# A two-layer graph network kernel: the weight sums, the scales and the second row tile are reordered in the first stage

## The chip, the cores and the metric

The kernel runs on one core of one Trainium2 chip. The metric is the device time of one execution in microseconds (us), the median over several executions. A core has five engines that run their own instruction streams and meet at semaphores: TensorE (PE, matrix products and transposes), VectorE (DVE), ScalarE (ACT), GpSimd (POOL) and SyncE (SP, which here only issues transfers).

## The reference

2500 nodes with 1024 features, 80,000 edges with weights, two 1024 x 1024 weight matrices:

```python
edge_index = jnp.stack([src, dst])
h = jnp.maximum(_layernorm(x, axis=-1), 0.0)
# first layer: support = h @ W0; out[dst] += support[src] * edge_weight
x = x + _L0_gnn_ref(h, L0_gnn_W, edge_weight, src, dst)
h = jnp.maximum(_layernorm(x, axis=-1), 0.0)
# second layer: (h @ W1.T + b), summed over edges and self loops, scaled by degrees
x = x + _L1_gnn_ref(h, edge_index, L1_gnn_W, L1_gnn_b)
return x
```

## The kernel before

The nodes are 20 row tiles of 128. The first stage computes, for each row tile t, `support = h @ W0`. A 32-bit factor is split into two 16-bit parts, a high one (`hi`) and what is left of it (`lo`), and each product is three: hi x hi, hi x lo, lo x hi. Later stages turn the edge list into dense 128-column weight tiles by one-hot products, multiply them with the support, and do the second layer in the same way. There is no planner: each engine's order is written out by hand, one block for each engine, and the order of the calls in a block is the order of the engine's queue.

The start of the kernel matters here. Its steps, with the names of the code:

- **SP** issues the load of tiles 0 and 1 of x (`load_x(0)`), of the edge weights, destinations and sources (640 for each of 125 partitions), of W0 in four pieces into `w_nat` (semaphores `w0nat_in`), and later the other groups of x.
- **DVE** computes the moments of tiles 0 and 1 (`moments(0)`, `scale_shift(0)`), the largest edge weight, and from the integer lists two fields `field[0]` and `field[1]`. Then it makes a power-of-two scale for the edge weights (`wscale`), the scaled edge weights `w_s` with the high part `w_hi` (`field[2]`) and the left-over `w_lo` (`field[3]`), and from the largest row sum of W0 a scale for W0 (`powers`, semaphore `w_pow`). For each of the eight blocks k of 128 rows of W0 it makes the low part (L890), when ACT has made the high part (L1483). After the eight, it runs two scans over one row (L896, L897, semaphore `scans_ready`), and the moments of tiles 4 to 7.
- **ACT** takes the square root of the variances (`std`), normalizes a row tile and makes its high part (`rows_normal`, L1411 and L1416), sums the absolute values of W0's rows (`weight_sums`, L1443), copies transposed tiles out of PSUM (`transposed`, L1423), copies transposed fields out of PSUM (`field_out`, L1455), and makes the high parts of W0 (L1483).
- **POOL** makes the low part of a normalized row tile (`h_left`, L687), and after the scans three conversions (L693 to L696) ahead of `h_left(2)`.
- **PE** transposes the row tiles (`transpose_rows`, L1617) and the fields (`turn_field`, L1592), turns a column of 128 maxima into a row (`spread_max`, L1577), sends a value to all partitions (`to_all`, L1582), computes the support (`support`, L1634: six products of 128x512 for each block k), and spreads the scans (`spread_scans`, L1604).

What PE does for tile 0 stands in this order:

```python
            for t in range(T):
                support(t, 0, 2)
                if t + 1 < T:
                    transpose_rows(t + 1)
                for k in range(2, KD):
                    support(t, k, k + 1)
                    if t == 0 and k == 2:
                        turn_field(3)
                    if t < 2 and k == KD - 1:
                        spread_scans(t)
```

Each `support(0, k, ...)` waits for `w0_lo`, the low part of block k. `spread_scans(0)` waits for the scans and for `field_out(2)`. `transpose_rows(t)` waits for `h_left(t)`.

## Time and profile before

| | before |
|---|---|
| median of 3 executions | 1483.26 us (1482.24 to 1484.04) |
| span of the profiled execution | 1480.6 us |
| PE busy | 1444.0 us, 98% of the span |
| DVE busy | 958.5 us, 65% |
| ACT busy | 441.1 us, 30% |
| POOL busy | 303.0 us, 20% |
| share of PE in the chain that ended last | 87% |

The span runs from the first to the last instruction of one profiled execution; no separate time outside the profiler is given for that execution. The median of the runs shown is 2.7 us above this span. Times in the rows are counted from the start of the span. A busy engine is one that has an instruction in flight. Neighbouring instructions overlap at their ends, so the start of the next one tells more than start plus duration.

### The profile page before, as it was taken

The page shows a single profiled execution, that of the slowest core. Times are in us where ns is not written, and L with a number is a line of the kernel's source. Part 1 is how long each engine was busy: PE and PEld are TensorE (multiplying, and loading weights), DVE is VectorE, ACT ScalarE, POOL GpSimd, SP SyncE. Part 2 cuts the span into 40 slices and gives each one's busy share as a digit, 9 for nine tenths or more (in the row PEclk, how much of TensorE's full clock was granted, in tenths as well). Part 3 has the DMA queues.
Part 4 walks back from the last instruction along what each step waited for, and adds up shares of the span by engine and source line. Part 5 has one row for each costly group of instructions (what it writes and reads, how often), then busy time and mean ns, then how long its engine had stood idle before and what let it go on. Part 6 is the DMA issues. An engine that isn't in the chain of part 4 may idle for free.

```text
span 1480.6 us, 24633 instructions
## 1 busy us (share of the span) xinstructions
PE 1444.0 (98%) x7580; PEld 766.2 (52%) x7581; DVE 958.5 (65%) x1732; ACT 441.1 (30%) x869; POOL 303.0 (20%) x578
## 2 busy tenths in 40 slices
PE   3989999999999999999999999999999999999999
PEld 2555555555555555555555544446446446446455
DVE  7788785767877866666665634986554554555542
ACT  7545554422222223322223313812011011021000
POOL 2244333323333333333333310000000000001000
PEclk9999999999999999999999999999999999999999
DMA  8301431237667788888888886804305105104002
GB/s 310 115 24 47 123 102 24 46 80 146 156 149 154 160 180 186 175 182 181 179 183 181 180 181 227 282 29 150 102 8 183 61 18 185 49 29 140 28 1 83
DMA packets 414350, 185.62 MB, mean 125 GB/s; under 512 B 379624, under 2 KB 396540, under 8 KB 414216
## 3 DMA queue, kind: packets, MB, share of 16 engines
q1 hardware_dynamic: 329736, 157.82, 42.0%
q10 hardware_dynamic: 84480, 26.22, 7.2%
q8 instruction: 59, 0.97, 0.3%
q14 instruction: 75, 0.61, 0.2%
HBM read 76.45 MB, written 77.11 MB: 104 GB/s over the span
## 4 chain that ended last, share of the span: by engine, by line
PE 87%; DVE 7%; DMA 2%; issue 2%; ACT 1%; SPq 1%; DVEq 0%; POOL 0%; ACTq 0%; POOLq 0%
PE pair L1750 28%; PE pair L1846 22%; PE pair L1902 13%; PE pair L1634 13%; PE pair L1646 7%; PE pair L1703 1%; PE pair L1617 1%; DVE slots L994 1%; DVE slots L995 1%; DMA h<-x_scratch 1%; DVE negbase L1316 1%; DMA wstage<-c_scratch 1%; DVE slots L989 0%; SPq L484 0%; DVE slots L991 0%
## 5 line engine op out<-in xcount | busy, mean ns | idle before, releaser
L1750 PE MATMUL pair<-h,area 128*128 128x512 f16 x2400 | 542.2, 379 | 0.5 <-issue 0.5
L1750 PEld LDWEIGHTS pair<-h,area 128*128 128x128 f16 x2400 | 233.8, 98 | 252.5 <-issue 2.2
L1846 PE MATMUL pair<-area,h 128*128 128x500 f16 x1600 | 339.1, 374 | 1.3 <-DVE h L1250 1.3
L1846 PEld LDWEIGHTS pair<-area,h 128*128 128x128 f16 x1600 | 155.5, 97 | 184.0 <-issue 2.2
L741 POOL TENSOR_TENSOR deg_acc<-deg_acc,area 128x320 f32<-128x320 f32 x160 | 151.8, 949 | 363.1 <-ACT area L1382 363.1
L1902 PE MATMUL pair<-wmat,area 128*125 128x512 f16 x960 | 209.0, 379 | 0.0
L1380 ACT ACTIVATE area<-pair 128x320 f32<-128x320 f32 x160 | 70.1, 438 | 425.2 <-PE pair L1646 416.6
L1902 PEld LDWEIGHTS pair<-wmat,area 128*125 128x125 f16 x960 | 130.6, 136 | 75.5
L1054 DVE SCALAR_TENSOR_TENSOR area<-pair,area 128x320 f16<-128x320 f32 x160 | 77.6, 485 | 133.6 <-ACT area L1382 112.1
L1646 PE MATMUL pair<-slots 128*128 128x240 f16 x1120 | 144.2, 267 | 7.2 <-DVE slots L995 6.1
L1646 PEld LDWEIGHTS pair<-slots 128*128 128x128 f16 x1120 | 108.8, 98 | 54.2 <-DVE slots L995 11.0
L1564 ACT ACTIVATE area<-pair,sc 128x500 f16<-128x500 f32 x40 | 27.1, 677 | 364.8 <-PE pair L1846 364.8
L1634 PE MATMUL pair<-wmat,agg_t 128*128 128x512 f16 x480 | 112.2, 384 | 3.1 <-DVE wmat L890 3.1
L1301 DVE SCALAR_TENSOR_TENSOR area<-pair,sc,area 128x500 f16<-128x500 f32 x40 | 29.3, 737 | 131.1 <-ACT area L1564 131.0
L1634 PE MATMUL pair<-wmat,xt 128*128 128x512 f16 x480 | 110.7, 382 | 0.0
L989 DVE TENSOR_TENSOR slots<-iota_r,fbuf 128x640 f16<-128x640 f16 x141 | 74.4, 528 | 49.5 <-PE pair L1646 19.6
L991 DVE TENSOR_TENSOR slots<-iota_r,fbuf 128x1024 f16<-128x1024 f16 x141 | 96.3, 683 | 0.0
L1057 DVE TENSOR_TENSOR area<-area 128x320 f16<-128x320 f16 x160 | 78.7, 492 | 5.5
L995 DVE TENSOR_TENSOR slots<-slots,fbuf 128x640 f16<-128x640 f16 x141 | 80.5, 571 | 0.0
L994 DVE TENSOR_TENSOR slots<-slots,fbuf 128x640 f16<-128x640 f16 x141 | 78.0, 553 | 0.0
L1634 PEld LDWEIGHTS pair<-wmat,agg_t 128*128 128x128 f16 x480 | 46.9, 99 | 54.3 <-issue 6.3
L1634 PEld LDWEIGHTS pair<-wmat,xt 128*128 128x128 f16 x480 | 46.7, 99 | 51.7 <-issue 1.8
(240 smaller groups left out, 1171.6 us busy)
## 6 DMA issues: line engine op xcount, KB each, us to landing
c_scratch<-area ACTq DMA_DIRECT2D x160, 160.0 KB, 3.0
a_scratch<-area SPq DMA_DIRECT2D x320, 80.0 KB, 2.4
xt<-in_x SPq DMA_DIRECT2D x19, 512.0 KB, 3.9
x_scratch<-xt SPq DMA_DIRECT2D x19, 512.0 KB, 3.4
xt<-x_scratch SPq DMA_DIRECT2D x20, 448.0 KB
out_x<-xt SPq DMA_DIRECT2D x19, 448.0 KB
wstage<-c_scratch SPq DMA_DIRECT2D x17, 500.0 KB, 4.2
slots<-c_scratch SPq DMA_DIRECT2D x17, 500.0 KB, 5.4
```

Of the source, the lines that this page charges most:

```text
L741: pool.tensor_tensor(deg_acc[:], deg_acc[:], c_stage(s), ALU.add).then_inc(win_sum, 1)
L989: nc.vector.tensor_tensor(part(hot(s), M0, SB), columns(8, SB), by_touch(s, 1, 8, SB), ALU.is_equal).then_inc(hots_plain, 1)
L991: nc.vector.tensor_tensor(part(hot(s), 0, P), columns(8, P), by_touch(s, 0, 8, P), ALU.is_equal)
L994: nc.vector.tensor_tensor(part(hot(s), W0C, SB), part(hot(s), M0, SB), by_touch(s, 2, 8, SB), ALU.mult)
L995: nc.vector.tensor_tensor(part(hot(s), W1C, SB), part(hot(s), M0, SB), by_touch(s, 3, 8, SB), ALU.mult).then_inc(hots_ready, 1)
L1054: nc.vector.scalar_tensor_tensor(a_stage(s)[:, 1], sums[:, :, SB:2 * SB], A_DOWN, a_stage(s)[:, 0], ALU.mult, ALU.subtract).then_inc(win_e ...
L1057: nc.vector.tensor_tensor(a_stage(s)[:, 1], a_stage(s)[:, 1], a_stage(s)[:, 2], ALU.add).then_inc(win_lo, 1)
L1634: last = pe.matmul(dest[:, half * H:(half + 1) * H], h_t(t)[:, q, k, :], wmat[:, r, k, half * H:(half + 1) * H], start=k == q == r == 0, s ...
L1646: return pe.matmul(dest, touches[:, t, 0:P], touches[:, t, P:CS], start=first, stop=last, skip_group_check=True)
L1750: last = pe.matmul(sum_pair(e)[:, half * H:(half + 1) * H], wts(e)[:, q, k, :], hpart(k, r)[:, half * H:(half + 1) * H], start=k == q == r ...
L1846: ins = pe.matmul(sums_of(c, f), hpart(k, q)[:, f * P:(f + 1) * P], counts, start=first and q == 0, stop=last and q == 1, skip_group_check ...
L1902: last = pe.matmul(out_pair(m)[0:RW, half * H:(half + 1) * H], agg_of(k, q)[:, b * RW:(b + 1) * RW], wmat[:, r, k, half * H:(half + 1) * H ...
```

## The change

- ACT: `rows_normal(1)` (tile 1) no longer stands ahead of the weight sums. It stands between blocks 1 and 2 of W0's high parts. `field_out(1)` moves from ahead of the high parts to behind block 0, `field_out(2)` from behind block 5 to behind block 6, `std(1)` from behind block 2 to behind block 7.
- DVE: the reduction of the weight sums moves ahead of the scale of the edge weights. Of the edge weights' work only `w_s` stays ahead of W0's scale; `w_hi`, `field[2]` and the subtraction come behind it, `w_lo` and `field[3]` come behind block 1 of the low parts. `moments(1)` moves from ahead of the eight low parts to behind block 3, `unscale` and `scale_shift(1)` behind block 7.
- PE: `spread_max(1)` comes ahead of `turn_field(0)`, `to_all(2)` between `turn_field(0)` and `turn_field(1)`. Then eight products of 128x512 are new (`WARM`), whose result nobody reads. `turn_field(2)` moves from ahead of the support to behind block 4 of tile 0, `transpose_rows(1)` from behind block 1 to behind block 5, with `turn_field(3)` behind it.
- A table's third register is read with an instruction of its own (`value_load`), in `window_table` on DVE and PE, and ACT's one register in `window_out` in the same way.

```diff
         def window_table(eng, regs, v):
-            eng.load(regs, wtab[0:1, bass.ds(v * 4, 3)])
+            eng.load(regs, wtab[0:1, bass.ds(v * 4, 2)])
...
-                    eng.snap(regs[2], min_val=0, max_val=MOST))
+                    eng.value_load(wtab[0:1, bass.ds(v * 4 + 2, 1)], min_val=0, max_val=MOST))
...
+        WARM = 8
...
             nc.vector.tensor_reduce(top[0:1, 1:2], bank[0][0:1, 0:EP], AX.X, ALU.max).then_inc(top_row, 1)
+            dve.wait_ge(w0_summed, KD)
+            nc.vector.tensor_reduce(top[:, 4:5], w_sums[:, 0, :], AX.X, ALU.max).then_inc(top_ready, 1)
 
             dve.wait_ge(top_all, 1)
...
-            chain(nc.vector.tensor_scalar(w_s, w_n, wscale[0:EP, 2:3], None, ALU.mult))
-            chain(nc.vector.tensor_copy(w_hi, w_s))
-            dve.wait_ge(w0_summed, KD)
-            nc.vector.tensor_reduce(top[:, 4:5], w_sums[:, 0, :], AX.X, ALU.max).then_inc(top_ready, 1)
-            chain(nc.vector.tensor_copy(field[2], w_hi))
-            chain(nc.vector.tensor_tensor(w_s, w_s, field[2], ALU.subtract))
             dve.wait_ge(top_tp, 2)
             nc.vector.tensor_reduce(top[0:1, 7:8], bank[0][0:1, 0:P], AX.X, ALU.max).then_inc(top_row, 1)
-            chain(nc.vector.tensor_copy(w_lo, w_s))
-            nc.vector.tensor_copy(field[3], w_lo).then_inc(fields_ready, 1)
+            chain(nc.vector.tensor_scalar(w_s, w_n, wscale[0:EP, 2:3], None, ALU.mult))
             dve.wait_ge(top_all, 2)
             powers(bank[1][:, 0:1], 2, 1)
             nc.vector.tensor_scalar(scale_of[:, 2:3], sc[:, 10:11], 2.0 ** 13, None, ALU.mult).then_inc(w_pow, 1)
-            chain(nc.vector.tensor_scalar(unscale[:, 0:1], low[:, 2:3], wscale[:, 3:4], 1.0 / SUP_UP, ALU.mult, ALU.mult))
-            moments(1)
+            chain(nc.vector.tensor_copy(w_hi, w_s))
+            chain(nc.vector.tensor_copy(field[2], w_hi))
+            chain(nc.vector.tensor_tensor(w_s, w_s, field[2], ALU.subtract))
             for k in range(KD):
                 dve.wait_ge(w0_hi, k + 1)
                 nc.vector.scalar_tensor_tensor(wmat[:, 1, k, :], w_nat[:, k, :], scale_of[:, 2:3], wmat[:, 0, k, :],
                                                ALU.mult, ALU.subtract).then_inc(w0_lo, 1)
+                if k == 1:
+                    chain(nc.vector.tensor_copy(w_lo, w_s))
+                    nc.vector.tensor_copy(field[3], w_lo).then_inc(fields_ready, 1)
                 if k == 3:
-                    scale_shift(1)
+                    moments(1)
+            chain(nc.vector.tensor_scalar(unscale[:, 0:1], low[:, 2:3], wscale[:, 3:4], 1.0 / SUP_UP, ALU.mult, ALU.mult))
+            scale_shift(1)
...
-                act.load(regs, wtab[0:1, bass.ds(n * 16 + 15, 1)])
-                through = act.snap(regs[0], min_val=1, max_val=MOST + 1)
+                through = act.value_load(wtab[0:1, bass.ds(n * 16 + 15, 1)], min_val=1, max_val=MOST + 1)
...
             rows_normal(0)
-            rows_normal(1)
...
             field_out(0)
-            field_out(1)
             act.wait_ge(w_pow, 1)
             for k in range(KD):
                 act.activation(wmat[:, 0, k, :], w_nat[:, k, :], ACT.Copy, scale=sc[:, 14:15]).then_inc(w0_hi, 1)
-                if k == 2:
-                    std(1)
-                if k == 5:
+                if k == 0:
+                    field_out(1)
+                if k == 1:
+                    rows_normal(1)
+                if k == 6:
                     field_out(2)
+            std(1)
...
             to_all(1, bank[1][:, 0:1], 1, 2)
+            spread_max(1, P, 4)
             turn_field(0)
+            to_all(2, bank[1][:, 0:1], 7, 8)
             turn_field(1)
-            spread_max(1, P, 4)
-            to_all(2, bank[1][:, 0:1], 7, 8)
+            pe.wait_ge(ht_ready, 2)
+            for _ in range(WARM):
+                pe.matmul(TP[:, 0:512], ident_u[:], h_t(0)[:, 0, 0:4, :].rearrange("p k d -> p (k d)"), start=True,
+                          stop=True)
             pe.wait_ge(etab_ready, 1)
             pe.wait_ge(w_pow, 1)
-            turn_field(2)
...
                 support(t, 0, 2)
-                if t + 1 < T:
+                if 0 < t < T - 1:
                     transpose_rows(t + 1)
...
-                    if t == 0 and k == 2:
+                    if t == 0 and k == 4:
+                        turn_field(2)
+                    if t == 0 and k == 5:
+                        transpose_rows(1)
                         turn_field(3)
```

## Rows read from the trace of the kernel before

**Rows 1.** The page's chain that ended last, shares of the span by engine.

```profile
PE 87%; DVE 7%; DMA 2%; issue 2%; ACT 1%; SPq 1%; DVEq 0%; POOL 0%; ACTq 0%; POOLq 0%
```

**Rows 2.** The same chain in order of time, 0 to 90 us: start, us, what.

```profile
30.89 4.96 PE pair L1634 x12
...
45.06 1.26 PE pair L1604 x4
46.32 2.70 PE pair L1634 x12
```

**Rows 3.** ACT's instructions in order: start, us, line, operation, out<-in, count.

```profile
12.04 1.23 ACT L1411 ACTIVATE h<-h,shift,scale 128x1024 f32<-128x1024 f32 x1
...
14.26 1.04 ACT L1443 ACTIVATE agg_t<-h 128x1024 f16<-128x1024 f32 x1
...
20.69 1.06 ACT L1443 ACTIVATE agg_t<-h 128x1024 f16<-128x1024 f32 x1
...
22.92 1.94 ACT L1423 ACTIVATE agg_t<-pair 128x1024 f16<-128x1024 f16 x2
24.74 2.78 ACT L1455 ACTIVATE etab<-pair 128x625 f32<-128x625 f32 x2
27.26 3.19 ACT L1483 ACTIVATE wmat<-h,sc 128x1024 f16<-128x1024 f32 x3
```

**Rows 4.** The four transfers of W0 (line 447): issue, and time to landing.

```profile
L447 SPq DMA_DIRECT2D h<-in_L_gnn_W x4: 390/470/472, 4.0 to 5.4; - x4
...
DMA to landing us min/median/max: 8.1/11.2/15.2
```

**Rows 5.** DVE's instructions in order, 0 to 100 us.

```profile
14.72 2.30 DVE L842 TENSOR_SCALAR area<-area 125x640 f32<-125x640 int32 x1
...
22.01 0.55 DVE L873 TENSOR_SCALAR area<-area,wscale 125x640 f32<-125x640 f32 x1
...
24.58 0.28 DVE L880 TENSOR_REDUCE top<-pair 1x1 f32<-1x128 f32 x1
24.79 0.47 DVE L881 CAST area<-area 125x640 f16<-125x640 f32 x1
...
25.70 0.15 DVE L865 TENSOR_SCALAR sc<-pair 128x1 f32<-128x1 f32 x1
...
26.57 2.47 DVE L812 BATCH_NORM_STATS2 stats<-h 128x6 f32<-128x512 f32 x4
...
29.47 4.87 DVE L890 SCALAR_TENSOR_TENSOR wmat<-h,sc,wmat 128x1024 f16<-128x1024 f32 x4
...
39.51 1.44 DVE L896 TENSOR_TENSOR_SCAN area<-area 1x625 f32<-1x625 f32 x1
...
42.23 4.81 DVE L812 BATCH_NORM_STATS2 stats<-h 128x6 f32<-128x512 f32 x8
```

**Rows 6.** PE's instructions in order; in brackets the idle time before.

```profile
24.91 0.58 PE L1582 MATMUL pair<-top,ones 1*128 1x1 f32 x2 [1.20 <-DVE top L880]
26.52 1.27 PE L1592 MATMUL pair<-ident,area 125*128 125x125 f32 x5 [1.03 <-DVE sc L885]
...
103.18 1.35 PE L1646 MATMUL pair<-slots 128*128 128x240 f16 x8 [2.94 <-DVE slots L995]
```

**Rows 7.** POOL's instructions in order, 0 to 100 us.

```profile
14.43 2.25 POOL L687 TENSOR_TENSOR xt<-h,xt 128x1024 f16<-128x1024 f32 x1
...
45.08 2.13 POOL L687 TENSOR_TENSOR agg_s<-h,agg_s 128x1024 f16<-128x1024 f32 x1
```

**Rows 8.** All of DVE's line 1062: ns min/median/max, first and last start.

```profile
L1062 DVE SCALAR_TENSOR_TENSOR wstage<-h,sc,wstage x16: 737/740/2116, 103.1 to 210.0; 128x512 f16<-128x512 f32 x16
```

**Rows 9.** DVE in order of time, 162.9 to 165.2 us.

```profile
163.05 2.77 DVE L1062 SCALAR_TENSOR_TENSOR wstage<-h,sc,wstage 128x512 f16<-128x512 f32 x2 [0.82 <-ACT wstage L1399]
```

**Rows 10.** POOL in order of time, 160 to 168 us.

```profile
162.48 2.13 POOL L687 TENSOR_TENSOR agg_s<-h,agg_s 128x1024 f16<-128x1024 f32 x1 [11.74 <-ACT agg_s L1416]
```

**Rows 11.** ACT's register reads at line 1371: ns min/median/max.

```profile
L1371 ACTq TENSOR_LOAD <-area x160: 273/278/1057, 87.9 to 866.7; - x160
```

More of the change, by code:

```diff
@@ L966, in _ @@
             nc.vector.tensor_reduce(top[:, 3:4], w_sums[:, 1, :], AX.X, ALU.max).then_inc(top_ready, 1)
-            regs = [dve.alloc_register(f"dve_window{i}") for i in range(3)]
+            regs = [dve.alloc_register(f"dve_window{i}") for i in range(2)]
             any_reg = [dve.alloc_register("dve_any")]
@@ L1365, in _ @@
         def _(act):
-            regs = [act.alloc_register("act_through")]
             def window_out(n, s, steps_done, pre=False):
-                act.load(regs, wtab[0:1, bass.ds(n * 16 + 15, 1)])
-                through = act.snap(regs[0], min_val=1, max_val=MOST + 1)
+                through = act.value_load(wtab[0:1, bass.ds(n * 16 + 15, 1)], min_val=1, max_val=MOST + 1)
                 pair = win_pair(s, pre)
@@ L1640, in _ @@
             pe.sem_inc(further_used, 1)
-            regs = [pe.alloc_register(f"pe_window{i}") for i in range(3)]
+            regs = [pe.alloc_register(f"pe_window{i}") for i in range(2)]
             any_reg = [pe.alloc_register("pe_any")]
```

## The prediction

> **What bounds the kernel now.** I read the page's chain first: PE holds 87% of it [rows 1], so what delays PE near the start delays everything behind it, unless a later wait swallows the delay. The same chain in order of time says where PE starts its products in earnest: the 12 products for blocks 0 and 1 of W0 at 30.89, the scans' spreading at 45.06, tile 1's products at 46.32 [rows 2]. The reader is to see two things there. Twelve products take 4.96 us the first time and 2.70 us the second time: the first ones run at 1.2 GHz, the later ones at 2.4 GHz. And between 30.89 and 46.32 PE never waits long: DVE makes a low part in 1.2 us (four in 4.87 [rows 5]), PE needs 1.3 us for a block (2.70 us for two [rows 2]). From 26.57 on I then read the three queues that feed PE: ACT, DVE, POOL [rows 3, 5, 7].
>
> **Part 1, ACT's weight sums.** Without rows_normal(1) (12.04 to 14.26, 2.2 us [rows 3]) the sums could start 2.2 us earlier. But the last quarter of W0 is issued at 5.4 and lands 15.2 later, at 20.6 [rows 4], and ACT starts on it at 20.69 [rows 3]. The two sums that need it end at 22.9 in either order. Worth nothing; the cover is that transfer. POOL's h_left(1) leaves 14.43, and DVE's L842, 2.30 us beside it, should take about 0.5 as L881 does on as many elements [rows 5, 7]. DVE gains 1.8 us, and then waits for the sums until 22.9 all the same: nothing.
>
> **Part 2, W0's scale.** From 22.93: reduction and PE's transposition 0.6, five one-column operations 0.9 (five stood between 25.70 and 26.57 [rows 5]), the second reduction 0.2 (L880 to L881 [rows 5]), L873 0.6, so DVE is ready at 24.8 to 24.9. PE's to_all(2) follows turn_field(0), five transposes at 0.21 [rows 6], at 24.4, and takes 0.6 [rows 6]: 25.0. Four one-column operations, 0.7: w_pow at 25.75. Before it came 0.7 behind 25.70, at 26.4. ACT copies the transposed tile until 24.74, then one field instead of two, 1.26 each [rows 3], and starts the first high part at 26.0 instead of 27.26.
>
> **Part 3, the first products.** DVE now puts three operations ahead of the first low part: w_hi, field[2] and the subtraction. They are what is left of 22.01 to 24.58 without L873 (0.6) and the small reduction (0.16) [rows 5]: 1.8. The first low part is made from 27.55 to 28.75; before, it ran from 29.5 to 30.7. PE: turn_field(1) ends at 25.95, eight spare products at 1.2 GHz cost 8 x 0.41 (4.96 / 12 [rows 2]) = 3.3, so the support starts at 29.3 instead of 30.89. Twelve products need between 2.7 (all at 2.4 GHz) and 5.0 (all at 1.2); before, the clock rose 4.5 us into the products, so I take it to rise near 30.5, and blocks 0 and 1 are done by 32.4, with bounds of 32.0 and 34.3. Before they were done at 35.85. Here the change leads by 3.4 us.
>
> **Part 4, what feeds blocks 2 to 7.** ACT: high part 0 to 27.03; field_out(1) 1.26 to 28.3; high part 1 to 29.35; rows_normal(1), 2.2, to 31.55; high part 2 to 32.6, then one each 1.03 (3.19 for three [rows 3]), the seventh at 36.7.
> DVE: low part 1 waits for ACT, 29.35 to 30.55; w_lo and field[3] 0.9 (24.79 to 25.70 [rows 5]) to 31.45. Low part 2 could start at 32.6. But POOL's h_left(1) now runs from 31.55 to 33.7 (2.13 [rows 7]), beside it. No row of L890 stands beside a POOL operation. The nearest is L1062, the same operation with the same kinds of operands, half as wide: 740 ns at the median, 2116 at most [rows 8]. At 163.05 two of them take 2.77 us [rows 9], while POOL holds from 162.48 to 164.61 [rows 10]: the first one ends 0.5 us after POOL. So low part 2 is blocked until 33.7 and ends at 34.95. The bounds are no blocking at all (33.8) and this; I take the blocking, since operation and operands are the same.
> The Trainium skill, "SBUF — State Buffer", section "SBUF: two separate sides", says that a VectorE operation with two inputs in SBUF and a GpSimd operation that reads SBUF exclude each other for the whole instruction. By that rule this part of the sum is +1.15 us, without it nothing.
> Low part 3 to 36.15. moments(1), 2.9 (26.57 to 29.47 [rows 5]), to 39.05; before, the same 2.9 stood where PE had nothing to do yet. Low part 4 to 40.3. PE has finished block 3 by 37.5 and waits 2.8 us. Block 4 to 41.6, turn_field(2) 0.5 (half of 26.52's five [rows 6], at 2.4 GHz) to 42.15. Only then can ACT copy this field, 42.3 to 43.55, and only behind that does it make high part 7, to 44.6. DVE, through with low part 6 at 42.7, waits 1.9 and ends low part 7 at 45.8. Before, it was at 39.5.
>
> **Part 5, what is late next.** unscale and scale_shift(1) 0.65 (the second from 29.47 to 39.51 less eight times 1.2 [rows 5]), scans 2.7 (39.51 to 42.23 [rows 5]): ready at 49.2. PE, finished with block 7 at about 47.5, waits for them; before, they were ready at 42.23 and PE came at 45.06 [rows 2]. That is +4.15. Behind the scans POOL does three conversions and h_left(2), which ended at 47.21 before, 5.0 behind the scans [rows 5, 7]: now 54.2. PE comes to transpose_rows(2) 3.96 behind the start of the spreading (1.26 + 2.70 [rows 2]), at 53.2, and waits 1.0 more. Tile 2's transposes start at 54.2 instead of 49.02: **+5.2 us**. From here on DVE and ACT follow PE's transposes and spreads as before, and I find no wait in the chain that would swallow 5 us. SP's load of W1 into w_nat waits for low part 7 as well, and starts 6 us later; ACT doesn't need it before tile 2, which is 5 us later too.
>
> **Part 6, the registers.** A read costs ACT 278 ns [rows 11], 160 of them in front of waits for PE; the new form is no more than one such read. In window_table it is one more, in a branch that the trace never enters (no operation of it stands there). Nothing; if all 160 ACT reads were doubled and on the path, 44 us, but ACT is 30% busy and waits for PE at these places.
>
> **The sum.** 30.89 to 49.02 becomes 5.2 longer: a span of 1485.8 against 1480.6. The same added to the median of the runs, which lies 2.7 above that span: 1483.26 + 5.2 = **1488.5**.
>
> **Rivals.**
> The waits for ACT and POOL don't appear (DVE alone sets the time). Then DVE's work from w_pow on is 25.75 + 1.8 + 9.6 + 0.9 + 2.9 + 0.65 + 2.7 = 44.3, PE isn't held at 45.06, h_left(2) ends at 49.3 against 49.02: +0.3, 1483.6. For it: my waits are 0.6, 2.2 and 1.9, each a small difference of long sums. Against: high part 7 hangs on turn_field(2), which hangs on low part 4 behind moments(1), by program order. 0.13.
> Only some of them: without the blocking +4.05, 1487.3; without the wait for h_left(2) as well +3.1. Such cases, still slower, have 0.17.
> The clock falls in the 2.8 us wait ahead of block 4. An idle PE of 2.94 us at 103.18 [rows 6] was followed by eight one-hot products of 1.35 us: half speed. Twelve products at half speed cost 2.3 more, and block 4 and turn_field(2) are on the path to high part 7: up to +7.5, 1490.8. 0.14.
> The lead is kept, the other side: the support starts early and at full rate, and nothing holds it later: -3.4, 1479.9. It decides at block 4, whose low part would have to be there at 35, and at the scans, needed by 41.6, where DVE's work alone comes to 44.3. Or the later fall of the clock behind 103.18 doesn't recur, up to -2.3. Together 0.10 for an end below 1480.3.
> My forecast itself, within about a microsecond: 0.46.
>
> **How the numbers follow.** 0.2% is 3.0 us, about what a measurement of this kernel can tell. Slower is the forecast, the partial cases and the clock: 0.77. Same is the DVE-only case with a little of the partial ones: 0.13. Faster 0.10. The range has the DVE-only case at its lower end (1483.6, rounded to 1484.0) and the fallen clock at the upper (1491.0). The likeliest case's own range is 1487.0 to 1490.0.
>
> **What the profile after would show.** Seventh weight sum still at 20.7. First product of the support near 29.3, blocks 2 and 4 each behind an idle PE (2.5 and 2.8 us) that L890 ends. The L890 beside POOL at 2.3 us instead of 1.2. field_out(2) between high parts 6 and 7, behind 42. L896 at 46.5 instead of 39.5, first L1604 near 49.2, an L1617 that waits for POOL, near 54.2. I am wrong if moments(1) finds a gap of PE's that costs nothing, or if something behind 49 us swallows the delay: then the first stage is longer and the span isn't.

## The result and the profile after

The changed kernel took 1488.99 us (median of 4 executions, 1487.72 to 1492.94) against 1483.11 us for the kernel before on the same chip: a ratio of 1.0044 [1.003, 1.0059], 5.9 us slower. A second comparison of the same two kernels, shown with the experiments, gave 1.0067 [1.0053, 1.0081]. The forecast was 1488.5. The sum agrees with the time, but several things that the sum doesn't have lie in it, with opposite signs.

The profiled execution took 1488.88 us with a span of 1487.1. First the start of the page, and the shares of the chain that ended last, where PE went from 87% [rows 1] to 93%:

```profile
span 1487.1 us, 24954 instructions
...
PE 93%; DVE 3%; ACT 2%; DMA 1%; issue 1%; SPq 0%; POOL 0%; DVEq 0%; ACTq 0%; POOLq 0%
```

The transfers of W0 in after (line 448), which answer to [rows 4]: the slowest lands 14.8 us after its issue instead of 15.2.

```profile
DMA to landing us min/median/max: 7.7/10.8/14.8
```

ACT's instructions in order, in after [rows 3]: start, us, line, what, and in brackets the idle time before.

```profile
20.25 1.06 ACT L1441 ACTIVATE agg_t<-h 128x1024 f16<-128x1024 f32 x1 [1.22 <-DMA h<-in_L_gnn_W]
...
25.50 1.13 ACT L1480 ACTIVATE wmat<-h,sc 128x1024 f16<-128x1024 f32 x1
...
28.75 1.23 ACT L1410 ACTIVATE h<-h,shift,scale 128x1024 f32<-128x1024 f32 x1
...
42.92 1.47 ACT L1453 ACTIVATE etab<-pair 128x625 f32<-128x625 f32 x1 [6.66 <-PE pair L1592]
44.15 1.10 ACT L1480 ACTIVATE wmat<-h,sc 128x1024 f16<-128x1024 f32 x1
```

The reader is to see that tile 1's normalization, now at 28.75, costs nothing where it was taken away: the sum at 20.25 still waits for the transfer. And ACT idles 6.66 us before it can copy field 2 (L1453), because PE turns that field late. The eighth high part stands behind it, at 44.15.

DVE's instructions in after [rows 5], and POOL's one beside them [rows 7]:

```profile
27.27 1.28 DVE L887 SCALAR_TENSOR_TENSOR wmat<-h,sc,wmat 128x1024 f16<-128x1024 f32 x1
...
32.14 3.40 DVE L887 SCALAR_TENSOR_TENSOR wmat<-h,sc,wmat 128x1024 f16<-128x1024 f32 x2 [1.04 <-ACT wmat L1480]
35.47 2.46 DVE L813 BATCH_NORM_STATS2 stats<-h 128x6 f32<-128x512 f32 x4
...
38.35 3.67 DVE L887 SCALAR_TENSOR_TENSOR wmat<-h,sc,wmat 128x1024 f16<-128x1024 f32 x3
45.29 1.29 DVE L887 SCALAR_TENSOR_TENSOR wmat<-h,sc,wmat 128x1024 f16<-128x1024 f32 x1 [3.26 <-ACT wmat L1480]
```

```profile
31.14 2.12 POOL L688 TENSOR_TENSOR xt<-h,xt 128x1024 f16<-128x1024 f32 x1 [16.83 <-DVE area L891]
```

The two low parts from 32.14 take 3.40 us, where the single ones take 1.28. The second is undisturbed at about 1.2, so the first took 2.2: it ended about 1.1 us after POOL's 33.26. Then the moments stand between low part 3 and low part 4, and the eighth low part comes at 45.29, 3.26 us after DVE was through with the seventh.

PE in after [rows 2, 6]; its windows row is from 39.60 to 43.70, with, behind the window's length, the busy time of PE, its weight loads, DVE, ACT and POOL, then the granted clock as a share of full speed, the DMA share and GB/s:

```profile
25.64 2.40 PE L1778 MATMUL pair<-agg_t,ident_u 128*128 128x512 f16 x8
28.70 2.99 PE L1634 MATMUL pair<-wmat,agg_t 128*128 128x512 f16 x12 [0.66 <-DVE wmat L887]
34.41 2.77 PE L1634 MATMUL pair<-wmat,agg_t 128*128 128x512 f16 x12 [2.72 <-DVE wmat L887]
39.69 2.16 PE L1634 MATMUL pair<-wmat,agg_t 128*128 128x512 f16 x6 [2.52 <-DVE wmat L887]
41.64 1.25 PE L1592 MATMUL pair<-ident,area 125*128 125x125 f32 x5
...
50.06 1.33 PE L1604 MATMUL pair<-area,ones 1*128 1x512 f32 x4 [1.37 <-DVE area L899]
...
54.95 1.07 PE L1617 MATMUL pair<-ident_u,agg_s 128*128 128x128 f16 x16 [0.86 <-POOL agg_s L688]
```

```profile
39.60:43.70 4.10, 4.01 (x14) 2.27 (x15) 2.42 (x3) 0.78 (x1) 0.00 (x0) 0.59 0.02 4
```

The same work in before, at full speed: six products, a turned field, and tile 2's transposes.

```profile
36.59 1.46 PE L1634 MATMUL pair<-wmat,agg_t 128*128 128x512 f16 x6
37.88 0.70 PE L1592 MATMUL pair<-ident,area 125*128 125x125 f32 x5
...
48.85 1.06 PE L1617 MATMUL pair<-ident_u,agg_s 128*128 128x128 f16 x16
```

The waits stand where the forecast put them: 2.72 us ahead of block 2, 2.52 ahead of block 4, one for the scans, one for POOL. In this execution the mean clock from 39.60 to 43.70 is 0.59 of full speed, because the trace's record has half speed from 40.32 to 43.73: block 4 took 2.16 us, where six products at 2.4 GHz take 1.46, and turning the field 1.25 instead of 0.70. Tile 2's transposes start at 54.95. In before they start at 48.85.

A caution on the clock of the first products: the granted clock has no record ahead of 35.40 in before and ahead of 26.67 in after, and a windows row prints 1.00 there. Their speed is read from their starts instead. In before neighbouring products of 128x512 start 0.43 us apart until about 35.1 and 0.22 us apart behind it; in after the spare products change from 0.43 to 0.22 at 26.8, next to the first record of full speed.

From here I compare the start of the same PE work in both traces. The shift is +6.1 us at tile 2's transposes, +6.5 at the start of tile 5, +5.7 from there to 190, +9.6 at the first dense tile near 205, +9.7 at 440, +8.0 from 522 on, and +6.5 at the end. So three more places have a say: one near 197 us, one between 454 and 522 (a wait in after that is 0.6 us longer, and behind it short gaps of before, 2.3 us together, that after doesn't have), and one in the second layer. Near 197, first three lines of after (PE, DVE, POOL in order of time), then the same three of before:

```profile
200.05 1.16 PE L1646 MATMUL pair<-slots 128*128 128x240 f16 x8 [3.23 <-DVE slots L997]
...
197.58 2.41 DVE L997 TENSOR_TENSOR slots<-slots,fbuf 128x640 f16<-128x640 f16 x1
...
197.35 2.29 POOL L688 TENSOR_TENSOR agg_s<-h,agg_s 128x1024 f16<-128x1024 f32 x1 [7.77 <-ACT agg_s L1415]
```

```profile
192.15 0.99 PE L1646 MATMUL pair<-slots 128*128 128x240 f16 x8 [1.06 <-DVE slots L995]
...
191.61 0.48 DVE L995 TENSOR_TENSOR slots<-slots,fbuf 128x640 f16<-128x640 f16 x1
...
191.62 2.46 POOL L687 TENSOR_TENSOR agg_s<-h,agg_s 128x1024 f16<-128x1024 f32 x1 [7.77 <-ACT agg_s L1416]
```

Before, DVE's last one-hot product and POOL's subtraction start within 0.01 us of each other; DVE goes first and takes 0.48 us. After, POOL starts 0.23 us ahead, DVE takes 2.41, and PE waits 3.23 instead of 1.06. In the text below this is **the tie**. The Trainium skill, "SBUF — State Buffer", section "SBUF: two separate sides", says that whichever of the two starts first has the shared ports for the whole instruction. By that rule the trace agrees on both sides: 0.48 when DVE starts first, 2.41 when POOL does.

In the second layer before waited where after doesn't. PE in before:

```profile
929.60 1.85 PE L1846 MATMUL pair<-area,h 128*128 128x500 f16 x8 [0.83 <-DVE h L1250]
...
931.91 4.38 PE L1846 MATMUL pair<-area,h 128*128 128x500 f16 x20 [0.47 <-DVE h L1250]
```

### The profile page after: what moved, and what is told of

Read it like the earlier page. It is cut to its first block, busy times and chain, and to the rows that moved or that the text cites. A ratio compares the mean times of both kernels' runs of the same rounds, so it can differ in the third digit from the quotient of the medians.

```text
span 1487.1 us, 24954 instructions
## 1 busy us (share of the span) xinstructions
PE 1445.3 (97%) x7588; PEld 768.8 (52%) x7589; DVE 949.6 (64%) x1732; ACT 441.6 (30%) x869; POOL 297.0 (20%) x578
## 4 chain that ended last, share of the span: by engine, by line
PE 93%; DVE 3%; ACT 2%; DMA 1%; issue 1%; SPq 0%; POOL 0%; DVEq 0%; ACTq 0%; POOLq 0%
PE pair L1750 34%; PE pair L1852 23%; PE pair L1908 13%; PE pair L1634 12%; PE pair L1646 8%; PE pair L1703 1%; DMA h<-in_L_gnn_W 1%; PE pair L1617 1%; DVE negbase L1318 1%; DVE slots L991 0%; DVE slots L997 0%; DVE wmat L887 0%; DVE slots L993 0%; ACT wstage L1441 0%; ACT etab L1453 0%
## 5 line engine op out<-in xcount | busy, mean ns | idle before, releaser
L742 POOL TENSOR_TENSOR deg_acc<-deg_acc,area 128x320 f32<-128x320 f32 x160 | 147.4, 921 | 374.8 <-ACT area L1381 374.8
L1303 DVE SCALAR_TENSOR_TENSOR area<-pair,sc,area 128x500 f16<-128x500 f32 x40 | 29.3, 738 | 130.4 <-ACT area L1564 130.2
L1059 DVE TENSOR_TENSOR area<-area 128x320 f16<-128x320 f16 x160 | 82.4, 515 | 5.5
L997 DVE TENSOR_TENSOR slots<-slots,fbuf 128x640 f16<-128x640 f16 x141 | 76.5, 543 | 0.0
L1318 DVE SCALAR_TENSOR_TENSOR negbase<-area,dinv,negbase 128x500 f32<-128x500 f16 x95 | 70.2, 739 | 2.5
```

Source lines behind the costliest of these rows:

```text
L742: pool.tensor_tensor(deg_acc[:], deg_acc[:], c_stage(s), ALU.add).then_inc(win_sum, 1)
L997: nc.vector.tensor_tensor(part(hot(s), W1C, SB), part(hot(s), M0, SB), by_touch(s, 3, 8, SB), ALU.mult).then_inc(hots_ready, 1)
L1059: nc.vector.tensor_tensor(a_stage(s)[:, 1], a_stage(s)[:, 1], a_stage(s)[:, 2], ALU.add).then_inc(win_lo, 1)
L1318: ins = nc.vector.scalar_tensor_tensor(s_acc, counts, dinv[:, k:k + 1], s_acc, ALU.mult, ALU.add)
```

## The experiments

Each kernel was compared with the kernel before on the same chip. The ratios are made over all executions that were compared, and can differ from the quotient of the medians by 0.001. T2 is the start of tile 2's transposes in its profile (before 48.85, after 54.95). Four kernels start from the changed one and alter one part each. They were measured beside the kernel before (median 1481.81 us) and not beside the changed one, so that their medians bear on it only through the ratios, 1.0044 and 1.0067 for the changed kernel.

**1. Tile 1 normalized early** (a_normal_early):

```diff
             rows_normal(0)
+            rows_normal(1)
...
-                if k == 1:
-                    rows_normal(1)
```

> The changed kernel with one part undone: tile 1 is normalized ahead of the weight sums again. My theory: ACT waited 1.6 us for W0's pieces there, so the first high part starts no later (25.5), high part 2 ends 2.2 us earlier, the subtraction on POOL no longer stands beside low part 2 (1.2 us instead of 2.2), L843 takes 2.3 us again without cost. Low part 4 ends near 37.6 instead of 39.6, the last low part near 43.2 to 44.5 instead of 46.5, tile 2's transposes start at 51.6 (52.9 if the clock falls ahead of block 4 again) instead of 54.95. About 3 us faster than the changed kernel, 3 us slower than the kernel before. Rival (the new place of the row tile is harmless, moments alone set the delay): tile 2's transposes stay within 0.5 us of 54.95.

Measured: 1487.98 us, ratio 1.0049 [1.0032, 1.0066]; T2 52.13. Two rows of DVE, in order of time:

```profile
31.07 2.48 DVE L887 SCALAR_TENSOR_TENSOR wmat<-h,sc,wmat 128x1024 f16<-128x1024 f32 x2
...
42.10 1.28 DVE L887 SCALAR_TENSOR_TENSOR wmat<-h,sc,wmat 128x1024 f16<-128x1024 f32 x1 [2.07 <-ACT wmat L1481]
```

Two low parts take 2.48 again, with POOL's subtraction out of the way, as they must if POOL held the first of them up; run 3 tests that alone. ACT's copy of W0 isn't late at the front (first high part at 25.57 against 25.50), so bringing the normalization back is free. But DVE still waits 2.07 for the eighth high part, which hangs on the turned field.

**2. The field turned early** (a_turn_early):

```diff
                 support(t, 0, 2)
+                if t == 0:
+                    turn_field(2)
...
-                    if t == 0 and k == 4:
-                        turn_field(2)
```

> The changed kernel with turn_field(2) behind block 1 of tile 0, where TensorE is idle, instead of behind block 4. My theory (high part 7 hung on block 4 through the field's copy): ACT copies the field at 36.3 and makes high part 7 by 38.7; the last low part follows the others, ends near 43.2 instead of 46.5; the scans are done near 46.7, tile 2's transposes start near 51.6 instead of 54.95. 3.3 us faster than the changed kernel. Rival (the scans are late through VectorE's own work, the field's place costs nothing): no change within 0.5 us.

Measured: 1486.79 us, ratio 1.0044 [1.0029, 1.0058]; T2 52.07. ACT in order of time: field_out(2) no longer waits, and the eighth high part comes at 37.84 instead of 44.15.

```profile
36.64 1.45 ACT L1453 ACTIVATE etab<-pair 128x625 f32<-128x625 f32 x1
37.84 1.10 ACT L1480 ACTIVATE wmat<-h,sc 128x1024 f16<-128x1024 f32 x1
```

T2 is 2.9 us earlier than in after. The clock has a part in that: here it fell at 35.32, in blocks 2 and 3, and not in block 4. Against the second profile of the changed kernel (run 5), where it fell at the same place, T2 is 1.6 us earlier. The mechanism is the forecast's: low part 4 behind the moments, block 4, the turn, the copy, high part 7.

**3. POOL held back** (a_pool_waits): the subtraction of tile 1 comes behind the fourth low part, with everything else as changed. It takes away the lock alone.

```diff
-            for t in range(2):
-                h_left(t)
+            h_left(0)
+            pool.wait_ge(w0_lo, 4)
+            h_left(1)
```

> The changed kernel, and GpSimd's subtraction for tile 1 waits until four low parts are made, so that it runs beside the batch statistics and not beside low part 2. My theory (the two operations exclude each other): both low parts 2 and 3 take 1.2 us, together 2.4 instead of 3.4, everything behind moves up by 1.0 us: tile 2's transposes at 53.9. GpSimd's operation takes 2.1 us beside the statistics, and these 2.5 us as before. Rival (low part 2 is slow for another reason, such as its place behind a wait): it still takes 2.2 us.

Measured: 1487.38 us, ratio 1.0045 [1.0028, 1.0061]; T2 52.88. DVE and POOL in order of time:

```profile
32.18 2.48 DVE L888 SCALAR_TENSOR_TENSOR wmat<-h,sc,wmat 128x1024 f16<-128x1024 f32 x2 [1.04 <-ACT wmat L1481]
34.58 2.46 DVE L814 BATCH_NORM_STATS2 stats<-h 128x6 f32<-128x512 f32 x4
...
34.74 2.13 POOL L688 TENSOR_TENSOR xt<-h,xt 128x1024 f16<-128x1024 f32 x1 [20.50 <-DVE wmat L888]
```

The lock cost 0.92 us (3.40 to 2.48). T2 came 2.1 earlier, not 0.9: here the clock didn't fall behind the wait for block 4, which gives the other 1.2. The moments run beside the same POOL operation at their usual 2.46.

I had expected these three kernels to be about 3, 3.3 and 1 us faster than the changed one. Their profiles show the earlier T2, but their ratios (1.0044 to 1.0049) can't be told from its 1.0044 and 1.0067. What the parts are worth in the median is shown by run 7 alone, which takes two of them away together.

**4. No spare products** (a_no_warm):

```diff
-        WARM = 8
+        WARM = 0
```

> The changed kernel without the eight spare products. My theory: blocks 0 and 1 take 4.9 us instead of 3.0 and end at 33.6, still ahead of low part 2 at 34.4; from there on the same as in the changed kernel, tile 2's transposes at 54.95 within 0.3 us (if the clock is as it was; up to 1.3 either way if not). Rival (the spare products carry a gain here too): about 2 us slower than the changed kernel.

Measured: 1492.02 us, ratio 1.0076 [1.0059, 1.0093]; T2 55.30. PE in order of time:

```profile
29.06 5.11 PE L1634 MATMUL pair<-wmat,agg_t 128*128 128x512 f16 x12 [2.85 <-DVE wmat L887]
34.76 2.76 PE L1634 MATMUL pair<-wmat,agg_t 128*128 128x512 f16 x12 [0.60 <-DVE wmat L887]
```

Without the spare products the first twelve take 5.11 us instead of 2.99, and the wait behind them shrinks from 2.72 to 0.60. All that the spare products win is waited away for low part 2. T2 hardly moves (0.35). The median is 4 to 5 us above those of the three kernels above, which its first stage doesn't explain. In its profile the clock falls at the same three places as in after's (40.69, 108.95 and 201.11 us). That profile ends 1.8 us behind after's: 0.35 is T2, and nearly all of the rest are the short gaps behind 454, which this trace has and after's doesn't. The mean granted clock of its four executions is 0.00125 below that of after's four. An estimate from that: a mean lower by 0.00125 over 1489 us is 3.7 us more at half the clock, which cost half of that, 1.9 us. Where the clock falls in the other three executions no trace shows, and with four executions of each, that it falls more often here isn't shown.

**5. The changed kernel again** (after_again), on another chip with the next three; before had 1481.13 us there.

> The changed kernel once more, beside the others on one chip. My theory: the same stage as in its first profile (tile 2's transposes at 54.95 within 0.5 us, two idle stretches ahead of blocks 2 and 4), 5 to 7 us slower than the kernel before. What is open is how much of the total comes from behind the first stage: its first profile has a longer wait near 197 us (3.2 instead of 1.0) with a fall of the clock behind it, and shorter waits later.

Measured: 1489.49 us, ratio 1.0067 [1.0053, 1.0081], 8.4 us. In this profile T2 is 53.65, +4.8: the clock fell at 34.99, in blocks 2 and 3, and the wait for low part 4 took that up (0.83 us of it were left, where after had 2.52). The shift is +4.7 at tile 5, +3.4 from there to the tie, because the clock doesn't fall behind the wait at 108.00, +7.2 behind the tie, +7.3 from 522 on, +5.6 at the end. The profiled execution was the fastest of the five (1487.91 us).

**6. The registers alone** (b_registers): before, with the new reads.

```diff
-            eng.load(regs, wtab[0:1, bass.ds(v * 4, 3)])
+            eng.load(regs, wtab[0:1, bass.ds(v * 4, 2)])
...
-                    eng.snap(regs[2], min_val=0, max_val=MOST))
+                    eng.value_load(wtab[0:1, bass.ds(v * 4 + 2, 1)], min_val=0, max_val=MOST))
...
-                act.load(regs, wtab[0:1, bass.ds(n * 16 + 15, 1)])
-                through = act.snap(regs[0], min_val=1, max_val=MOST + 1)
+                through = act.value_load(wtab[0:1, bass.ds(n * 16 + 15, 1)], min_val=1, max_val=MOST + 1)
```

> The kernel before with the change's register reads alone. My theory in the prediction: nothing, within 1 us. Rival, formed on the changed kernel's profile: ACT runs 160 more assertions ahead of its window copies, and somewhere a near tie between VectorE and GpSimd is decided the other way, as near 191 us, where the wait of TensorE grows from 1.0 to 3.2 us and the clock falls after it; then 2 to 4 us slower, and the wait of 3.2 us stands in this profile too, with the first stage untouched (tile 2's transposes at 48.85).

Measured: 1479.58 us, ratio 0.9989 [0.998, 0.9998], 1.6 us faster. T2 is 48.65 and the tie is as before. PE's two waits at 929 are gone. What is late there in before can be followed back over DVE and ACT to SP's queue. SP of before, then of b_registers:

```profile
880.80 1.50 SPq L519 DMA_DIRECT2D x_scratch<-xt  x1
885.16 0.31 SPq L526 DMA_DIRECT2D xt<-in_x  x1
```

```profile
880.52 0.58 SPq L519 DMA_DIRECT2D x_scratch<-xt  x1
883.88 0.31 SPq L526 DMA_DIRECT2D xt<-in_x  x1
```

The store of the last rows keeps SP for 1.50 us instead of 0.58, SP's next load is issued 1.3 us later, and all loads of the second layer follow it. All the other profiles of the study, all with the new reads, show 0.58. That the reads do this to SP's queue, whose code they don't touch, isn't shown: there is one profile of before. In the counts of instructions only ACT's differ: 160 assertions and 72 register operations more. In all thirteen profiles with the new reads PE gains 1.3 to 1.8 us at this place. The gain in the medians is small, but its interval excludes 1.

**7. Both waits undone** (a_both): 1 and 2 together.

> The changed kernel with tile 1 normalized ahead of the weight sums and turn_field(2) behind block 1 of tile 0: the waits for ACT and GpSimd are gone, and the first stage is VectorE's own work. My theory, the bound of the prediction's first rival (VectorE alone): low parts end near 41.5, scans are done near 45, tile 2's transposes start near 49.5, against 48.85 before and 54.95 in the changed kernel; what remains against the kernel before is about +0.6 us in this stage. Rival (some other part of the change is slow as well): over 51.

Measured: 1483.66 us, ratio 1.0018 [1.0009, 1.0027]; T2 49.61. PE in order of time:

```profile
44.71 1.33 PE L1603 MATMUL pair<-area,ones 1*128 1x512 f32 x4 [0.22 <-DVE area L899]
...
49.61 1.07 PE L1616 MATMUL pair<-ident_u,agg_s 128*128 128x128 f16 x16 [0.87 <-POOL agg_s L688]
```

The spreading starts 0.3 us earlier than in before (44.99), T2 is 0.8 later. This is the forecast's rival in which DVE alone sets the time, put at +0.3. The changed kernel on the same chip had 1489.49 us, so the two edits together gain 5.8 us, and the stage's 5 to 6 us are explained. Yet the kernel is 2.5 us slower than before, and 4.1 us slower than with the registers alone. The profile shows the tie lost here too (a wait of 3.24).

**8. Another order of the stage** (v_mix), an attempt at a faster one, from b_registers: six spare products, the moments of tiles 2 and 3 (`moments(1)`) behind all low parts, the scans spread and tile 2 transposed in the middle of tile 1's products, and some smaller moves. Of its diff the core:

```diff
+                    if t == 1 and k == 3:
+                        spread_scans(0)
+                        transpose_rows(2)
...
-                if k == 3:
-                    scale_shift(1)
+            moments(1)
+            scale_shift(1)
```

> A mix that the findings point to: the order of the kernel before with six spare products; both casts of the left-over edge weights behind W0's scale, the statistics of tiles 2 and 3 behind all eight low parts, GpSimd's subtraction for tile 2 ahead of its conversions, the first spreading of the scans between blocks 3 and 4 of tile 1, the statistics of tiles 4 to 7 behind the comparison with the first scan. My theory: TensorE starts the support near 28.5 at full rate and has no wait in tiles 0 and 1; tile 2's products start near 54.1 instead of 58.87 before: 4 to 5 us faster than the kernel before. Rival (a new wait takes the place of the old ones, likeliest for GpSimd's subtraction ahead of tile 2's transposes): tile 2's products start at 57 or later, under 2 us faster.

Measured: 1483.82 us, ratio 1.0017 [1.0008, 1.0026]: 4.2 us slower than with the registers alone. PE, the first products of tile 2:

```profile
54.39 2.76 PE L1630 MATMUL pair<-wmat,agg_t 128*128 128x512 f16 x12
```

Tile 2's products start 4.5 us ahead of before (58.87), and nothing of it is left at tile 5 (104.45 against 104.33): PE waits 0.98 at 65.8 and 1.83 at 83.1 for DVE's work on the table. A lead of PE in the first stage is given back, because DVE is as late as ever. The tie is lost here as well.

**9. One more semaphore instruction** (b_shift). The last product stands in a group of four that DVE runs without a pause. Where the tie is won, the group starts 1.40 to 1.43 us ahead of POOL's subtraction; where it is lost, 1.16 to 1.18, after 0.16 us of idle time that waits for nothing. In the traces of the losing kernels 375 DVE instructions stand in front of the group, in the others 374. So b_registers got one wait more that is long met, at 21 us:

```diff
+            dve.wait_ge(edges_in, 96)
             dve.wait_ge(top_all, 1)
```

> The kernel before with the change's register reads and one more semaphore instruction on VectorE at 21 us (a second wait, long fulfilled). What it tells apart: why TensorE's wait near 191 us is 1.04 us in the kernels of the old order and 3.2 us in every kernel with a reordered first stage. In those the instruction ahead of the late one-hots (L989) is VectorE's 375th record instead of the 374th, and starts 0.24 us later against GpSimd's subtraction. Theory A (the 0.24 us belong to the instruction's place in VectorE's stream, one semaphore instruction further on): here too L989 starts 1.17 us ahead of the subtraction instead of 1.41, the last one-hot product loses the tie, and TensorE waits 3.2 us near 191; first stage unchanged (48.65); about 2 us slower than with the register reads alone. Theory B (it comes from the order of the work itself): 1.04 us as in the kernel before.

Measured, with before at 1482.23 us here and in the next three: 1483.57 us, ratio 1.0006 [0.9997, 1.0015], where the same kernel without the wait had 0.9989 [0.998, 0.9998]. DVE, POOL and PE in order of time:

```profile
191.32 0.49 DVE L990 TENSOR_TENSOR slots<-iota_r,fbuf 128x640 f16<-128x640 f16 x1 [0.16 <-issue]
...
192.74 2.41 DVE L996 TENSOR_TENSOR slots<-slots,fbuf 128x640 f16<-128x640 f16 x1
...
192.51 2.29 POOL L687 TENSOR_TENSOR agg_s<-h,agg_s 128x1024 f16<-128x1024 f32 x1 [7.77 <-ACT agg_s L1414]
...
195.20 0.99 PE L1644 MATMUL pair<-slots 128*128 128x240 f16 x8 [3.23 <-DVE slots L996]
```

One wait that costs 0.08 us where it stands loses the tie 170 us later, worth 2.2 us of PE's wait. The two profiles differ in one more place: T2 is 49.56 here and 48.65 in b_registers. The support starts 0.24 us later, and the first record of full speed is at 36.57 instead of 34.97. So the 2.5 us between the two ratios needn't be the tie alone.

**10. One semaphore instruction less** (both_less): a_both, with one move that saves one in the chain of small operations.

```diff
                     chain(nc.vector.tensor_copy(w_lo, w_s))
+                    chain(nc.vector.tensor_scalar(unscale[:, 0:1], ...))
                     nc.vector.tensor_copy(field[3], w_lo).then_inc(fields_ready, 1)
...
-            chain(nc.vector.tensor_scalar(unscale[:, 0:1], ...))
             scale_shift(1)
```

> The kernel with tile 1 normalized early and turn_field(2) behind block 1, and unscale moved between w_lo and field[3], which saves VectorE one semaphore instruction (374 again instead of 375). Theory A (place in the stream): TensorE's wait near 191 us is 1.04 us again instead of 3.21, about 2 us faster than without this edit, equal to the kernel before within 1 us; tile 2's transposes at 49.6 to 49.9. Theory B (the order of the work): 3.2 us as before this edit.

Measured: 1480.3 us, ratio 0.999 [0.9981, 0.9999]; T2 50.34. DVE, POOL and PE in order of time:

```profile
191.66 0.48 DVE L997 TENSOR_TENSOR slots<-slots,fbuf 128x640 f16<-128x640 f16 x1
...
191.68 2.46 POOL L688 TENSOR_TENSOR agg_s<-h,agg_s 128x1024 f16<-128x1024 f32 x1 [7.77 <-ACT agg_s L1415]
...
192.21 0.99 PE L1645 MATMUL pair<-slots 128*128 128x240 f16 x8 [1.05 <-DVE slots L997]
```

The tie is won again, by 0.02 us, and the new order is as fast as b_registers although its T2 is 1.7 us later. In its profile the clock never falls behind the wait at 104.69, where that of before does [rows 6]. From a_both's profile to this one PE's work ends 4.9 us earlier: 2.2 are the tie, 1.5 the clock near 104, 1.9 the gaps between 454 and 522, less 0.7 for a later start of everything. Runs 9 and 10 move the tie in both directions by one instruction, and the fourteen profiles fall without exception into 374 and won (5) or 375 and lost (9). So the tie is shown as a cause, with 2.2 us; the whole difference of the medians isn't its own.

**11. Spare products in the old order** (b_warm): b_registers and eight spare products.

```diff
             to_all(2, bank[1][:, 0:1], 7, 8)
+            pe.wait_ge(ht_ready, 2)
+            for _ in range(8):
+                pe.matmul(TP[:, 0:512], ident_u[:], ..., start=True, stop=True)
             pe.wait_ge(etab_ready, 1)
```

> The kernel before with the change's register reads and its eight spare products alone. My theory: the clock is up when the support starts, blocks 0 and 1 take 2.7 to 3.0 us instead of 5.0, and in this order VectorE is ahead of TensorE (low parts every 1.2 us), so the gain stays until GpSimd's subtraction for tile 2 holds it: tile 2's transposes at 47.2 instead of 48.65. VectorE's stream keeps its length, the wait near 191 stays at 1.04. 1.4 us faster than with the register reads alone, 2 to 3 us faster than the kernel before. Rival (the spare products only delay turn_field(2) and gain nothing): tile 2's transposes at 48.5 or later.

Measured: 1479.02 us, ratio 0.9971 [0.996, 0.9983], the lowest of the study and below both kernels. But its profile doesn't show the mechanism. PE in order of time:

```profile
25.73 3.60 PE L1775 MATMUL pair<-agg_t,ident_u 128*128 128x512 f16 x8
...
31.20 4.53 PE L1631 MATMUL pair<-wmat,agg_t 128*128 128x512 f16 x12 [0.84 <-DVE wmat L890]
```

The eight products start 0.43 us apart, as at 1.2 GHz, and so do most of the twelve behind them; the first record of full speed is at 34.83 us, against 34.97 in b_registers. T2 is 48.73, where I had expected 47.2. That profiled execution (1480.37 us) was the slowest of its seven, so the others may have had the clock earlier; no trace shows it. Its interval overlaps that of b_registers, so that the spare products add anything isn't shown.

**12. POOL's order swapped at tile 4** (b_warm_swap), against the wait of 2.94 us in [rows 6]: the one-hot fields ahead of the subtraction of tile 6.

```diff
                 w = t - STEP0
+                if t + 2 < T and w > 0:
+                    h_left(t + 2)
                 if w < PQ:
                     if w + 1 < PQ:
                         fields_of(w + 1)
+                        if w == 0:
+                            h_left(t + 2)
```

> The last one, and in tile 4 GpSimd makes the fields for the next window ahead of its subtraction for tile 6, which stood beside VectorE's one-hots at 99.2 (2.1 us instead of 0.5) ahead of TensorE's longest late wait, 2.9 us, and a fall of the clock. Theory: that wait shrinks to about 1.7 us and the clock doesn't fall there: 1 to 3 us faster than the last one. Rival: the subtraction meets the next one-hots instead, and the time stays within 1 us.

Measured: 1482.98 us, ratio 1.0007 [0.9998, 1.0016]. PE in order of time:

```profile
101.55 0.99 PE L1645 MATMUL pair<-slots 128*128 128x240 f16 x8 [1.51 <-DVE slots L997]
...
110.29 1.89 PE L1616 MATMUL pair<-ident_u,agg_s 128*128 128x128 f16 x16 [4.93 <-POOL agg_s L687]
```

The wait of 2.94 becomes 1.51, and PE then waits 4.93 for the subtraction that was put back: a wait takes the place of the one removed, and the kernel is 4.0 us slower than b_warm.

## Why the prediction was right, step by step

| step | forecast | after | second profile or experiment |
|---|---|---|---|
| last weight sums end | 22.9 | 22.4 | the transfer landed 0.4 earlier |
| first high part | 26.0 | 25.50 | |
| support starts | 29.3 | 28.70 | |
| lock of low part 2 | +1.15 | 2.2 instead of 1.28 | +0.92 (run 3) |
| wait ahead of block 4 | 2.8 | 2.52 | |
| field_out(2) starts | 42.3 | 42.92 | |
| scans ready, spreading | 49.2 | 50.06 | 46.87 and 47.18 (runs 1, 2) |
| T2 | 54.2 | 54.95 | 53.65 (run 5) |
| DVE waits for high part 7 | 1.9 | 3.26 | 2.07 (run 1) |
| spare products | 3.3 | 2.40 | |
| DVE alone | +0.3 | | +0.8 (run 7) |

Parts 1 to 5 hold up to T2: each wait is at its place, PE's two waits for low parts are within 0.3 us of their size, and runs 1, 2 and 7 show that the delay comes from the parts that the forecast names. DVE's wait for high part 7 was forecast too small (1.9 for 3.26), because block 4 and the turned field ran at half speed; in run 1, where they ran at full speed, it is 2.07. The lock was put at 1.15 and cost 0.92. The spare products were put at 3.3 us and took 2.40. I had taken the clock to rise near 30.5, 4.5 us into PE's work as in before; full speed is on record from 26.67, 1.0 us into the spare products, so that reading of before doesn't carry over. It changed nothing, since the first product then waited 0.66 for low part 0. Against the T2 of 48.85 in the trace the stage costs 4.8 to 6.1 us, where I had 5.2. The spread between these two is the clock: the rival in which it falls in the wait ahead of block 4 came true in one of two profiles, at 1.2 us instead of the 2.3 that I had allowed, since only block 4 and the turned field ran slowly.

Two terms behind T2 were wrong. Part 6, "Nothing", is mis-sized: the new reads alone make the kernel 1.6 us faster (run 6); the profile shows that gain in the second layer, by way of SP's queue, but not why. And Part 5's "From here on DVE and ACT follow PE's transposes and spreads as before" is wrong at the tie, where 2.2 us of wait are added, and in both profiles of the changed kernel a fall of the clock right behind it (1.7 us). [rows 9] had shown me the same lock at 163.05, and I had asked only what stands beside W0's low parts. I hadn't looked for places in the later trace where DVE and POOL start almost together. What each place adds to the shift of PE's work, in the two profiles of the changed kernel against the one of before:

| place | after | after_again |
|---|---|---|
| T2 | +6.1 | +4.8 |
| clock near 103 to 109 us | -0.4 | -1.4 |
| the tie | +2.2 | +2.2 |
| clock behind the tie | +1.7 | +1.7 |
| waits and short gaps, 454 to 522 us | -1.7 | 0.0 |
| second layer | -1.5 | -1.7 |
| end | +6.5 | +5.6 |

Only the first row is in the forecast. The others come to +0.4 and +0.8, because they nearly cancel: that the sum is so near is in part luck. The 8.4 us of the second comparison isn't explained by this: its profiled execution is the fastest of its five, and the mean clocks of the others go down to 0.993, at places that no trace shows.

The side that I gave a chance of 0.10, a lead kept, is ruled out for this order by run 4: the lead of the spare products is worth 2 us at block 1 and nothing behind low part 2. The later fall of the clock behind 103.18 was absent in the second profile (1.4 us against before) and in those of a_pool_waits and both_less, so it does vary.

Left open: how the registers' reads act; why the short gaps between 454 and 522 are missing in the profiles of after, a_turn_early, both_less and b_warm_swap and not in the others; and what decides if the clock falls behind a wait. Bringing back `moments(1)` alone wasn't tried.

## What to carry to other kernels

Ahead of reordering an engine's queue, write down for each moved operation what the next engine makes of it and what that waits for: here the late turn of the field cost 1.6 to 2.9 us of T2, while moving the normalization and adding the spare products brought nothing. A lead of the busiest engine in the first stage is kept only if the engines that feed it come earlier too. And when two orders differ by some 2 us in 1480, look through the whole trace for places where two engines that share a resource start within a few tenths of a microsecond, before explaining it by the edit.

## What the hardware showed that I hadn't expected

- One semaphore instruction more on DVE at 21 us shifts a group of DVE's operations near 190 us by 0.24 us against POOL's. The other kernels with one more (8 in all) have the same shift, and it is gone in the one where it is taken out again. The profile puts 0.16 us of it down to "issue". Why it is kept over 170 us in which DVE waits for others many times, no row shows.
- A difference of 0.24 us in the start of two operations decides between 0.48 and 2.41 us for one of them.
- The wait of 2.52 us ahead of block 4 is the same in after, a_no_warm, a_normal_early, a_pool_waits, a_both and both_less. Behind it the products ran at 1.2 GHz in the first two profiles and at 2.4 GHz in the other four. The length of the idle time doesn't decide it alone.
- Eight spare products raised the clock before the support in the changed order (2.40 us for the eight in after), and didn't in b_warm's profile (3.60 us), though the same eight products started within 0.1 us of the same time. Ahead of them PE had worked without a gap from 22.68 on in after; in b_warm it had idled 1.20 us until 25.21. Whether that decides it, no run shows.
